# Attention on one core: value matmuls of two key tiles in one burst, and the quad sums in a shared four-bank ring

## The chip, the cores and the metric

The kernel runs on one core of one Trainium2 chip. The metric is the device time of one execution in microseconds (us); three executions of the kernel before took 3316.76, 3317.17 and 3322.76 us, with a median of 3317.17 us.

## The reference

Two conditional blocks run one after the other on x of shape (2, 2048, 512): a state space layer with a feed-forward block, then a 16-head self-attention block with conditional layer norms. Only the attention is touched here:

```python
B, N, D = hidden.shape                       # 2, 2048, 512
hd = D // num_heads                          # 16 heads of 32
h = _sln(hidden, w, ln_g, ln_b, Wg, bg, Wb, bb)
qkv = (h @ Wqkv.T + bqkv).reshape(B, N, num_heads, hd, 3)
energy = jnp.einsum('bhqd,bhkd->bhqk', q, k)
att = jax.nn.softmax(energy, axis=-1) / D ** 0.5
out = jnp.einsum('bhqk,bhkd->bhqd', att, v)
out = out @ Wp.T + bp
h1 = out + hidden
return _sln(h1, w, ...) + h1
```

## The kernel before, in words

The program is a row of stages: preparation, state space, feed-forward, query/key/value projection, attention, output projection. The attention stage (`attention_stage`, L1381) starts at about 1434 us and ends at about 3160 us of the profile.

It works through 32 blocks. A block is a group of four heads (`HG`), one of the two batches and a chunk of 512 queries (`CH`). It walks over 16 key tiles of 128 keys (`NKT`), so there are 512 tiles in all. Per tile:

- TensorE makes four scores (`score`, L1563), one per head, 128 keys by 512 queries, each in one of three PSUM banks (`SC`). A fourth score waits until ScalarE has read the first.
- ScalarE exponentiates each score into `probs` in SBUF (L1639; six tile buffers, `NPROB`).
- TensorE multiplies the exponentials of two tiles ago (`AV_LAG` = 2) with the values (`weigh`, L1575): four matmuls with 32 output columns each, side by side in the four column groups, that add up in PSUM bank `OUT` over the block. The profile shows each of these plain f32 matmuls as two instructions.
- GpSimd adds the exponentials of two tiles (`pair`, L1727), and a DMA on its queue that adds into its target folds two pairs into a quad (L1734). Nine tiles after the first tile of a quad (`SUM_LAG`), TensorE multiplies the quad with a matrix of ones (`total`, L1586), again four narrow matmuls, that add up in PSUM bank `DEN`. These are the sums of the softmax.

For the block that follows, TensorE also searches the maximum of each query's scores: `search` (L1548) makes 64 score tiles of 128 queries by 512 keys per block, in a ring of three PSUM banks (`MX`), and VectorE reduces each to a column (`find`, L1664). A search that needs a bank waits until the reduction three before it is done. After the last, the maxima are reduced (L1669), turned by TensorE (`turn`, L1554) and negated by VectorE (`negate`, L1674); the negated row goes with the queries as a further row of the score matmul. The searches run ahead of the scores: five a tile over the first twenty tiles and four a tile from there (`searched`), so the last 21 tiles have none.

The order of TensorE's work is written out: per tile score, search, score, search, `weigh` of two tiles before (and `total`, where one is due), score, search, score, search. Once a block, ScalarE copies `OUT` to SBUF (`copy_out`, L1624, in the second tile of the following block) and `DEN` to SBUF (`copy_sums`, L1629); VectorE turns the sums, inverts them and turns them back (L1681, L1685, L1689, after the finds of tiles 7, 8 and 9); GpSimd multiplies (L1715), and SyncE stores (L1487). The engines wait for each other by counting semaphores only.

Of the kernel before, what the change touches and what calls it, by code (L numbers as in the profile page):

```python
# [1380 lines left out]
def attention_stage(nc, sb, sem, psum, a, ident, wp, first, q_dram, k_dram, v_dram, att_dram):  # L1381
# [16 lines left out]
    MAXES = HG * TT * NKC  # L1398
    UNITS = HG * NKT

    AV_LAG, SUM_LAG = 2, 9
    RATE, AHEAD, TURN_KT = 4, 20, 12
    FIRST_TURN = 14

# [6 lines left out]
    part_max, maxima = first["part_max"], first["maxima"]  # L1411
    rows = sb("att_rows", [HG * TT, P], F32R)
    o_sum, den, att = sb("o_sum", [P, CH]), sb("den", [P, CH]), sb("att", [P, CH])
    inv = sb("den_inverse", [P, CH // HD])

    k_ld = [[sem(f"k_ld{b}{half}") for half in range(2)] for b in range(B)]
# [7 lines left out]
    o_copied, den_copied, den_turned, att_ready = (sem(n) for n in ("o_copied", "den_copied", "den_turned", "att_ready"))  # L1424
    inverted, spread = sem("den_inverted"), sem("inverse_spread")

    SC, MX, OUT, DEN = 0, 3, 6, 7

    def place(count):

# [11 lines left out]
    def searched(tile):  # L1442

        return min((RATE + 1) * tile, RATE * tile + AHEAD, MAXES * (BLOCKS - 1))

    def turn_of(tile):

        if tile == FIRST_TURN:
            return 1
        if tile % NKT == TURN_KT and 1 < tile // NKT + 1 < BLOCKS:  # L1450
            return tile // NKT + 1
        return None

    with nc.Block() as block:
# [73 lines left out]
        def _(pe):  # L1528
            items = [0]

            def ring_slot():

                number = items[0]
                items[0] += 1
                if number >= 3:
                    pe.wait_ge(max_read, number - 2)
                return psum[:, MX + number % 3, :]

            def search(s):

# [37 lines left out]

            def total(quad):

                count, r = quad // QUADS, quad % QUADS
# [27 lines left out]
            for tile in range(BLOCKS * NKT, BLOCKS * NKT + SUM_LAG):  # L1609
                if tile < BLOCKS * NKT + AV_LAG:  # L1610
                    weigh(tile - AV_LAG)
                if (tile - SUM_LAG) % 4 == 0:
                    total((tile - SUM_LAG) // 4)

        @block.scalar
        def _(act):
            act.sem_inc(o_copied, 1)
            act.sem_inc(den_copied, 1)
# [7 lines left out]
            def copy_sums(count):  # L1626

                act.wait_ge(sums_ready, QUADS * (count + 1))
                act.activation(den[:, :], psum[:, DEN, :], ACT.Copy).then_inc(den_copied, 1)  # L1629

            for tile in range(BLOCKS * NKT):
                count, kt = tile // NKT, tile % NKT
                if tile >= NPROB:
                    act.wait_ge(av_ready, tile - NPROB + 1)
                    act.wait_ge(pair_ready, (tile - NPROB) // 2 + 1)
                for h in range(HG):
                    unit = HG * tile + h
                    act.wait_ge(sc_ready, unit + 1)
                    act.activation(probs[tile % NPROB][:, h, :], psum[:, SC + unit % 3, :], ACT.Exp).then_inc(exp_ready, 1)  # L1639
                    if count > 0 and kt == AV_LAG - 1 and h == 2:  # L1640
                        copy_out(count - 1)
                if count > 0 and kt == SUM_LAG - 4:
                    copy_sums(count - 1)
            copy_out(BLOCKS - 1)
            copy_sums(BLOCKS - 1)

        @block.vector
        def _(dve):
            dve.memset(ones[:, :], float(D) ** 0.5).then_inc(consts, 1)
            items = [0]  # L1650

            def ring_slot():

                number = items[0]
                items[0] += 1
                dve.wait_ge(max_ready, number + 1)
                return psum[:, MX + number % 3, :]

            def find(s):
                count, j = s // MAXES + 1, s % MAXES  # L1660
                kc, qt, h = j // (HG * TT), j // HG % TT, j % HG
                if j == 0 and count > 1:
                    dve.wait_ge(max_final, count - 1)
                dve.tensor_reduce(part_max[:, h * TT + qt, kc:kc + 1], ring_slot(), AX.X, ALU.max).then_inc(max_read, 1)  # L1664
                if j == MAXES - 1:
                    dve.wait_ge(max_read, items[0])
                    if count > 1:
                        dve.wait_ge(neg_ready, count - 1)
                    dve.tensor_reduce(maxima[:, 0:HG * TT], part_max[:, :, :], AX.X, ALU.max).then_inc(max_final, 1)  # L1669

            def negate(count):
                if count > 1:
                    dve.wait_ge(row_ld, 16 * (count - 1))
                dve.tensor_scalar(rows[:, :], ring_slot()[0:HG * TT, 0:P], -1.0, None, ALU.mult).then_inc(neg_ready, 1)  # L1674
                dve.wait_ge(neg_ready, count)
                dve.sem_inc(max_read, 1)

            def turn_sums(count):
                dve.wait_ge(den_copied, count + 2)
# [12 lines left out]
            for tile in range(BLOCKS * NKT):  # L1692
                count, kt = tile // NKT, tile % NKT
                if turn_of(tile) is not None:
                    negate(turn_of(tile))
                for s in range(searched(tile), searched(tile + 1)):
                    find(s)
                if count > 0 and kt == 7:
                    turn_sums(count - 1)
                if count > 0 and kt == 8:  # L1700
                    invert(count - 1)
                if count > 0 and kt == 9:
                    spread_inverse(count - 1)
            turn_sums(BLOCKS - 1)
            invert(BLOCKS - 1)
            spread_inverse(BLOCKS - 1)

        @block.gpsimd
        def _(pool):
# [315 lines left out]
```

## Time and profile before

| | |
|---|---|
| median of three executions | 3317.17 us (3316.76 to 3322.76) |
| span of the profiled execution, from its first to its last instruction | 3319.1 us |
| TensorE matmuls busy | 3080.5 us (93%), 15333 instructions |
| VectorE busy | 2030.3 us (61%) |
| ScalarE busy | 1549.5 us (47%) |
| GpSimd busy | 1715.2 us (52%) |
| VectorE: searches reduced (L1664) | 1984, 681 ns each |
| ScalarE: exponentials (L1639) | 2048, 597 ns each |
| GpSimd: pair additions (L1727) | 256, 4580 ns each |
| TensorE: value matmuls (L1575) | 4096 instructions, 605 ns each |
| TensorE: sum matmuls (L1586) | 1024 instructions, 596 ns each |

The profile gives no time for the profiled execution apart from its span. Instructions of one engine overlap in part: four exponentials of 0.60 us each can lie within 2.11 us. So starts and ends are the safer reading, and for TensorE the starts alone, since the ends of its matmuls are modelled. In a row, "x4" joins that many instructions that follow each other.

### The profile page before, as it was taken

The numbers are of one execution on the slowest core, as the hardware profiler recorded it, in microseconds if no ns is written. First come the engines' busy times: TensorE is split into PE (matmuls) and PEld (weight loads), VectorE is DVE, ScalarE is ACT, GpSimd is POOL, SyncE is SP. The second block draws the span as 40 slices with busy tenths as digits, with TensorE's granted clock in tenths as the row PEclk, the third lists the DMA queues.
The fourth block names the chain that finished last, engine by engine and source line by source line (L and its number), as shares of the span: only waits on it lengthen the run. The fifth ranks groups of instructions, "written<-read, shape, count | busy, mean of one in ns | idle before, by whom it ended". The sixth has DMA issues, their size and how long they took to land. (4 is left out here: it accounts for less than half of the span.)

```text
span 3319.1 us, 42021 instructions
## 1 busy us (share of the span) xinstructions
PE 3080.5 (93%) x15333; PEld 1944.4 (59%) x15333; DVE 2030.3 (61%) x3514; ACT 1549.5 (47%) x2770; POOL 1715.2 (52%) x698
## 2 busy tenths in 40 slices
PE   4786999999998898989999999999999999999876
PEld 2665778777777676755454455544454554545355
DVE  7885222222221544668777777777777777777158
ACT  2232222222222232246666666666666666666622
POOL 2665301111110110137777777777777777777845
PEclk7887999999999899999999999999999999999988
DMA  6223100000000446364456654467444665444444
GB/s 239 98 102 119 40 26 25 25 25 25 25 13 16 169 171 181 115 170 101 95 106 145 147 110 91 102 143 156 96 102 102 147 132 115 102 94 97 99 169 151
DMA packets 134808, 347.68 MB, mean 105 GB/s; under 512 B 10295, under 2 KB 28219, under 8 KB 117866
## 3 DMA queue, kind: packets, MB, share of 16 engines
q1 hardware_dynamic: 116204, 211.20, 21.1%
q0 software_dynamic: 18432, 134.23, 19.9%
q8 instruction: 103, 1.69, 0.2%
q14 instruction: 69, 0.57, 0.1%
HBM read 135.34 MB, written 75.53 MB: 64 GB/s over the span
## 5 line engine op out<-in xcount | busy, mean ns | idle before, releaser
L1664 DVE TENSOR_REDUCE part_max<-psum 128x1 f32<-128x512 f32 x1984 | 1240.1, 681 | 356.2 <-PE psum L1548 350.6
L1727 POOL TENSOR_TENSOR pair<-probs 128x2048 f32<-128x2048 f32 x256 | 1172.6, 4580 | 393.0 <-ACT probs L1639 392.8
L1639 ACT ACTIVATE probs<-psum 128x512 f32<-128x512 f32 x2048 | 1090.7, 597 | 588.4 <-PE psum L1563 585.2
L1563 PE MATMUL psum<-queries,keys 97*128 97x512 f32 x2048 | 864.1, 425 | 9.4 <-PEq L1128 5.2
L1548 PE MATMUL psum<-keys,queries 96*128 96x512 f32 x1984 | 797.0, 402 | 5.4 <-DMA queries<-q_parts 5.4
L1563 PEld LDWEIGHTS psum<-queries,keys 97*128 97x128 f32 x2048 | 386.3, 189 | 501.1 <-ACT probs L1639 326.7
L1575 PE MATMUL psum<-probs,values 128*32 128x512 f32 x4096 | 545.4, 605 | 0.0
L1548 PEld LDWEIGHTS psum<-keys,queries 96*128 96x128 f32 x1984 | 376.8, 190 | 108.4 <-DVE part_max L1664 35.7
L980 DVE TENSOR_TENSOR h_lo<-w_stage,h_hi 128x512 fp32r<-128x512 f32 x128 | 96.8, 756 | 528.3 <-ACT h_hi L918 528.3
L1024 POOL TENSOR_TENSOR ffn_u_lo<-ffn_u,ffn_u_hi 128x512 fp32r<-128x512 f32 x32 | 41.2, 1287 | 554.0 <-DVE ffn_u_hi L970 554.0
L911 ACT ACTIVATE w_stage<-psum,b_col 128x512 f32<-128x512 f32 x128 | 88.1, 689 | 510.4 <-PE psum L38 510.4
L36 PE MATMUL psum<-ffn_u_hi,w_hi 128*128 128x512 f32 x512 | 203.9, 398 | 6.4 <-DVE b_parts L1006 6.4
L36 PE MATMUL psum<-w_hi,h_hi 128*128 128x512 f32 x512 | 203.5, 398 | 0.0
L38 PE MATMUL psum<-ffn_u_lo,w_hi 128*128 128x512 f32 x512 | 202.9, 396 | 0.0
L37 PE MATMUL psum<-ffn_u_hi,w_lo 128*128 128x512 f32 x512 | 202.9, 396 | 0.0
L37 PE MATMUL psum<-w_hi,h_lo 128*128 128x512 f32 x512 | 202.8, 396 | 0.0
L38 PE MATMUL psum<-w_lo,h_hi 128*128 128x512 f32 x512 | 202.2, 395 | 0.0
L1575 PEld LDWEIGHTS psum<-probs,values 128*32 128x32 f32 x4096 | 80.6, 108 | 179.3 <-issue 165.0
L1371 POOL TENSOR_TENSOR qkv_u_lo<-qkv_u,qkv_u_hi 128x512 fp32r<-128x512 f32 x32 | 41.2, 1287 | 263.7 <-DVE qkv_u_hi L1316 263.7
L1586 PE MATMUL psum<-pair,att_ones 128*32 128x512 f32 x1024 | 134.3, 596 | 13.5 <-DMA pair<-pair 13.5
L1734 POOL DMA_DIRECT2D pair<-pair x128 | 110.8, 865 | 45.5 <-POOL pair L1727 35.9
L1266 ACT ACTIVATE qk_hi<-psum,bqkv_col 128x512 fp32r<-128x512 f32 x64 | 44.0, 688 | 168.4 <-PE psum L38 151.6
(312 smaller groups left out, 3700.0 us busy)
## 6 DMA issues: line engine op xcount, KB each, us to landing
pair<-pair POOLq DMA_DIRECT2D x128, 1024.0 KB, 7.0
queries<-q_parts SPq DMA_DIRECT2D x96, 256.0 KB, 4.8
keys<-k_parts SPq DMA_DIRECT2D x42, 512.0 KB, 7.3
x<-in_x_dram SPq DMA_DIRECT2D x8, 1024.0 KB, 7.4
y<-in_x_dram SPq DMA_DIRECT2D x8, 1024.0 KB, 5.6
y_rows<-y SPq DMA_DIRECT2D x8, 1024.0 KB, 5.1
qkv_z<-z_rows SPq DMA_DIRECT2D x8, 1024.0 KB, 5.8
q_parts<-qk_hi SPq DMA_DIRECT2D x32, 256.0 KB, 2.1
```

The costliest lines, as they stand in the source:

```text
L36: nc.tensor.matmul(out, w_hi, x_hi, start=first, stop=False)
L37: nc.tensor.matmul(out, w_lo, x_hi, start=False, stop=False)
L38: return nc.tensor.matmul(out, w_hi, x_lo, start=False, stop=last)
L980: dve.tensor_tensor(h_lo[j % NH][:, :], g[j % 2], h_hi[j % NH][:, :].bitcast(F32), ALU.subtract).then_inc(glo_ready, 1)
L1548: nc.tensor.matmul(ring_slot(), queries[count % NQ][0:R, h, qt * P:(qt + 1) * P], keys[b][0:R, h, kc * CH:(kc + 1) * CH], start=True, stop ...
L1563: nc.tensor.matmul(psum[:, SC + unit % 3, :], keys[place(count)[0]][0:R + 1, h, kt * P:(kt + 1) * P], queries[count % NQ][0:R + 1, h, :], ...
L1575: mm = nc.tensor.matmul(psum[h * HD:(h + 1) * HD, OUT, :], values[b][:, kt, h * HD:(h + 1) * HD], probs[tile % NPROB][:, h, :], start=(kt ...
L1586: mm = nc.tensor.matmul(psum[h * HD:(h + 1) * HD, DEN, :], ones[:, :], pair[(2 * quad + 1) % NPAIR][:, h, :], start=(r == 0), stop=(r == Q ...
L1639: act.activation(probs[tile % NPROB][:, h, :], psum[:, SC + unit % 3, :], ACT.Exp).then_inc(exp_ready, 1)
L1664: dve.tensor_reduce(part_max[:, h * TT + qt, kc:kc + 1], ring_slot(), AX.X, ALU.max).then_inc(max_read, 1)
L1727: pool.tensor_tensor(pair[number % NPAIR][:, :, :], probs[2 * number % NPROB][:, :, :], probs[(2 * number + 1) % NPROB][:, :, :], ALU.add) ...
L1734: pool.dma_start(pair[number % NPAIR][:, :, :], pair[(number - 1) % NPAIR][:, :, :], accum_op=ALU.add).then_inc(folded, 16)
```

## The change

```diff
-    AV_LAG, SUM_LAG = 2, 9
+    AV_LAG, SUM_LAG = 3, 11
+    DIRECT = QUADS * BLOCKS - 2
+    summed = sb("summed", [P, CH])
-    SC, MX, OUT, DEN = 0, 3, 6, 7
+    SC, MX, OUT = 0, 3, 7
+    NMX = 4
 (ring_slot of TensorE)
-                if number >= 3:
-                    pe.wait_ge(max_read, number - 2)
-                return psum[:, MX + number % 3, :]
+                if number >= NMX:
+                    pe.wait_ge(max_read, number - NMX + 1)
+                return psum[:, MX + number % NMX, :]
 (total)
-                pe.wait_ge(folded, 16 * (quad + 1))
-                if r == 0:
-                    pe.wait_ge(den_copied, count + 1)
-                for h in range(HG):
-                    mm = nc.tensor.matmul(psum[h * HD:(h + 1) * HD, DEN, :], ones[:, :], pair[(2 * quad + 1) % NPAIR][:, h, :],
-                                          start=(r == 0), stop=(r == QUADS - 1))
+                direct = quad >= DIRECT
+                if not direct:
+                    pe.wait_ge(folded, 16 * (quad + 1))
+                    addends = [pair[(2 * quad + 1) % NPAIR]]
+                elif quad < QUADS * BLOCKS - 1:
+                    pe.wait_ge(pair_ready, 2 * quad + 2)
+                    addends = [pair[2 * quad % NPAIR], pair[(2 * quad + 1) % NPAIR]]
+                else:
+                    pe.wait_ge(pair_ready, 2 * quad + 1)
+                    pe.wait_ge(exp_ready, UNITS * BLOCKS)
+                    addends = [pair[2 * quad % NPAIR], probs[(4 * quad + 2) % NPROB], probs[(4 * quad + 3) % NPROB]]
+                slot = ring_slot()
+                for n, addend in enumerate(addends):
+                    for h in range(HG):
+                        mm = nc.tensor.matmul(slot[h * HD:(h + 1) * HD, :], ones[:, :], addend[:, h, :],
+                                              start=(n == 0), stop=(n == len(addends) - 1))
 (order of TensorE's work in a tile, after the second search)
-                        if tile >= AV_LAG:
-                            weigh(tile - AV_LAG)
-                        if tile >= SUM_LAG and (tile - SUM_LAG) % 4 == 0:
-                            total((tile - SUM_LAG) // 4)
-                        for s in found[HG:]:
-                            search(s)
+                        if tile % 2 == 1 and tile >= AV_LAG:
+                            weigh(tile - 3)
+                            weigh(tile - 2)
+                        if quad_of(tile) is not None:
+                            total(quad_of(tile))
+                for s in found[HG:]:
+                    search(s)
 (after the last tile)
+            weigh(BLOCKS * NKT - 2)
+            total(QUADS * BLOCKS - 2)
+            weigh(BLOCKS * NKT - 1)
+            total(QUADS * BLOCKS - 1)
 (ScalarE: copy_sums and its calls are gone; VectorE)
+            def gather(quad):
+                count, r = quad // QUADS, quad % QUADS
+                dve.wait_ge(sums_ready, quad + 1)
+                slot = ring_slot()
+                if r == 0:
+                    if count > 0:
+                        dve.wait_ge(den_turned, count)
+                    dve.tensor_copy(summed[:, :], slot).then_inc(max_read, 1)
+                else:
+                    dve.wait_ge(max_read, last_sum[0])
+                    dve.tensor_tensor(summed[:, :], slot, summed[:, :], ALU.add).then_inc(max_read, 1)
+                last_sum[0] = items[0]
-                dve.transpose(att[:, :], den[:, :]).then_inc(den_turned, 1)
+                dve.transpose(att[:, :], summed[:, :]).then_inc(den_turned, 1)
+                for s in found[0:2]:
+                    find(s)
+                if quad_of(tile) is not None:
+                    gather(quad_of(tile))
+                for s in found[2:]:
+                    find(s)
 (GpSimd: the last pair is not added, the last two quads are not folded)
-            for number in range(PAIRS * BLOCKS):
+            for number in range(PAIRS * BLOCKS - 1):
-                if p % 2 == 1:
+                if p % 2 == 1 and quad < DIRECT:
```

Here `quad_of(tile)` is the quad whose sum is due in a tile: `(tile - 11) // 4` where `tile % 4 == 3`, from tile 11 on. The values are weighed in the odd tiles, two tiles at a time. The quad sum goes into the next bank of the ring, which now has four banks, and VectorE adds it to `summed` in SBUF, between the second and the third find of the tile.

## Rows read from the trace of the kernel before

**Rows 1.** Busy us of PE, PEld, DVE, ACT, POOL in 500 us; clock, DMA.
```profile
1500.00:2000.00 500.00, 498.83 (x2716) 248.97 (x2715) 391.11 (x649) 326.05 (x619) 387.49 (x122) 1.00 0.55 116
```
**Rows 2.** Waits, 1500 to 3100 us: who for whom, us in total, times, longest.
```profile
ACT probs L1639 <- PE psum L1563: 548.8, 481, 3.5
DVE part_max L1664 <- PE psum L1548: 338.7, 415, 3.1
PEld psum L1586 <- DMA pair<-pair: 9.1, 6, 2.3
```
**Rows 3.** Timeline of TensorE: start, us, engine, line, operation; tiles in steady state.
```profile
2001.44 1.06 PE L1575 MATMUL psum<-probs,values 128*32 128x512 f32 x8
2002.44 0.50 PE L1563 MATMUL psum<-queries,keys 97*128 97x512 f32 x1
2002.78 0.40 PE L1548 MATMUL psum<-keys,queries 96*128 96x512 f32 x1
...
2004.19 0.39 PE L1548 MATMUL psum<-keys,queries 96*128 96x512 f32 x1
2004.51 1.07 PE L1575 MATMUL psum<-probs,values 128*32 128x512 f32 x8
...
2010.64 1.06 PE L1575 MATMUL psum<-probs,values 128*32 128x512 f32 x8
...
2014.56 1.06 PE L1575 MATMUL psum<-probs,values 128*32 128x512 f32 x8
```
**Rows 4.** Timeline of ScalarE and VectorE after the first of these bursts.
```profile
2002.98 2.11 ACT L1639 ACTIVATE probs<-psum 128x512 f32<-128x512 f32 x4 [0.51 <-PE psum L1563]
2003.21 2.48 DVE L1664 TENSOR_REDUCE part_max<-psum 128x1 f32<-128x512 f32 x4 [0.58 <-PE psum L1548]
```
**Rows 5.** Timeline of ScalarE where it copies the block's output.
```profile
1986.81 0.60 ACT L1639 ACTIVATE probs<-psum 128x512 f32<-128x512 f32 x1 [1.81 <-PE psum L1563]
...
1987.78 1.59 ACT L1639 ACTIVATE probs<-psum 128x512 f32<-128x512 f32 x3
```
**Rows 6.** Timeline of VectorE where it turns the sums.
```profile
2007.48 0.70 DVE L1681 STREAM_TRANSPOSE att<-den 128x512 f32<-128x512 f32 x1
2008.11 2.52 DVE L1664 TENSOR_REDUCE part_max<-psum 128x1 f32<-128x512 f32 x4
```
**Rows 7.** Timeline around the turn of the maxima, TensorE and VectorE.
```profile
2017.62 1.06 PE L1575 MATMUL psum<-probs,values 128*32 128x512 f32 x8
...
2020.59 0.27 DVE L1674 TENSOR_SCALAR att_rows<-psum 16x128 fp32r<-16x128 f32 x1
...
2021.01 1.29 DVE L1664 TENSOR_REDUCE part_max<-psum 128x1 f32<-128x512 f32 x2
2021.16 1.06 PE L1575 MATMUL psum<-probs,values 128*32 128x512 f32 x8
```
**Rows 8.** Groups by line and shape, VectorE additions and products in other stages.
```profile
L632 DVE TENSOR_TENSOR prod<-scan,s_sin 128x512 f32<-128x512 f32 x16 | 27.2, 1699 | 0.0
L1905 DVE TENSOR_TENSOR p_h<-psum,p_z 128x512 f32<-128x512 f32 x32 | 20.9, 685 | 29.5 <-PE psum L38 29.3 <-issue 0.2
```
**Rows 9.** Timeline of TensorE in the last block, which has no searches.
```profile
3126.32 0.96 PE L1563 MATMUL psum<-queries,keys 97*128 97x512 f32 x3
...
3127.51 0.49 PE L1563 MATMUL psum<-queries,keys 97*128 97x512 f32 x1 [0.23 <-ACT probs L1639]
...
3127.93 1.06 PE L1575 MATMUL psum<-probs,values 128*32 128x512 f32 x8
```
**Rows 10.** Timeline of the end of the attention stage.
```profile
3140.89 2.08 PE L1575 MATMUL psum<-probs,values 128*32 128x512 f32 x16
...
3141.93 4.52 POOL L1727 TENSOR_TENSOR pair<-probs 128x2048 f32<-128x2048 f32 x1 [0.42 <-ACT probs L1639]
...
3153.75 1.94 PE L1586 MATMUL psum<-pair,att_ones 128*32 128x512 f32 x8 [8.83 <-DMA pair<-pair]
3155.76 0.60 ACT L1629 ACTIVATE den<-psum 128x512 f32<-128x512 f32 x1 [12.13 <-PE psum L1586]
```

More of the change, by code:

```diff
@@ L1423, in attention_stage @@
     max_ready, max_read, max_final, neg_ready = (sem(n) for n in ("max_ready", "max_read", "max_final", "neg_ready"))
-    o_copied, den_copied, den_turned, att_ready = (sem(n) for n in ("o_copied", "den_copied", "den_turned", "att_ready"))
+    o_copied, den_turned, att_ready = (sem(n) for n in ("o_copied", "den_turned", "att_ready"))
     inverted, spread = sem("den_inverted"), sem("inverse_spread")
-    SC, MX, OUT, DEN = 0, 3, 6, 7
+    SC, MX, OUT = 0, 3, 7
+    NMX = 4
     def place(count):
@@ L1444, in searched, with quad_of @@
         return min((RATE + 1) * tile, RATE * tile + AHEAD, MAXES * (BLOCKS - 1))
+    def quad_of(tile):
+        return (tile - SUM_LAG) // 4 if tile >= SUM_LAG and (tile - SUM_LAG) % 4 == 0 else None
     def turn_of(tile):
@@ L1579, in total @@
             def total(quad):
-                count, r = quad // QUADS, quad % QUADS
-                pe.wait_ge(folded, 16 * (quad + 1))
-                if r == 0:
-                    pe.wait_ge(den_copied, count + 1)
-                for h in range(HG):
-                    mm = nc.tensor.matmul(psum[h * HD:(h + 1) * HD, DEN, :], ones[:, :], pair[(2 * quad + 1) % NPAIR][:, h, :],
-                                          start=(r == 0), stop=(r == QUADS - 1))
+                direct = quad >= DIRECT
[14 more added lines that the diff above has]
+                                              start=(n == 0), stop=(n == len(addends) - 1))
                 mm.then_inc(sums_ready, 1)
@@ L1602, in _ @@
                     if h == 1:
-                        if tile >= AV_LAG:
-                            weigh(tile - AV_LAG)
-                        if tile >= SUM_LAG and (tile - SUM_LAG) % 4 == 0:
-                            total((tile - SUM_LAG) // 4)
-                        for s in found[HG:]:
-                            search(s)
[L1609 to L1613, printed above, removed]
+                        if tile % 2 == 1 and tile >= AV_LAG:
[9 more added lines that the diff above has]
+            total(QUADS * BLOCKS - 1)
         @block.scalar
@@ L1617, in _ @@
             act.sem_inc(o_copied, 1)
-            act.sem_inc(den_copied, 1)
             def copy_out(count):
@@ L1624, in copy_out @@
                 act.activation(o_sum[:, :], psum[:, OUT, :], ACT.Copy).then_inc(o_copied, 1)
-            def copy_sums(count):
-                act.wait_ge(sums_ready, QUADS * (count + 1))
-                act.activation(den[:, :], psum[:, DEN, :], ACT.Copy).then_inc(den_copied, 1)
             for tile in range(BLOCKS * NKT):
@@ L1639, in _ @@
                     act.activation(probs[tile % NPROB][:, h, :], psum[:, SC + unit % 3, :], ACT.Exp).then_inc(exp_ready, 1)
-                    if count > 0 and kt == AV_LAG - 1 and h == 2:
+                    if count > 0 and kt == 1 and h == 2:
                         copy_out(count - 1)
-                if count > 0 and kt == SUM_LAG - 4:
-                    copy_sums(count - 1)
             copy_out(BLOCKS - 1)
-            copy_sums(BLOCKS - 1)
         @block.vector
@@ L1649, in _, with max_slot @@
             dve.memset(ones[:, :], float(D) ** 0.5).then_inc(consts, 1)
-            items = [0]
+            items, maxed, last_sum = [0], [0], [0]
             def ring_slot():
-                number = items[0]
                 items[0] += 1
-                dve.wait_ge(max_ready, number + 1)
-                return psum[:, MX + number % 3, :]
+                return psum[:, MX + (items[0] - 1) % NMX, :]
+            def max_slot():
+                maxed[0] += 1
+                dve.wait_ge(max_ready, maxed[0])
+                return ring_slot()
             def find(s):
@@ L1663, in find @@
                     dve.wait_ge(max_final, count - 1)
-                dve.tensor_reduce(part_max[:, h * TT + qt, kc:kc + 1], ring_slot(), AX.X, ALU.max).then_inc(max_read, 1)
+                dve.tensor_reduce(part_max[:, h * TT + qt, kc:kc + 1], max_slot(), AX.X, ALU.max).then_inc(max_read, 1)
                 if j == MAXES - 1:
@@ L1673, in negate @@
                     dve.wait_ge(row_ld, 16 * (count - 1))
-                dve.tensor_scalar(rows[:, :], ring_slot()[0:HG * TT, 0:P], -1.0, None, ALU.mult).then_inc(neg_ready, 1)
+                dve.tensor_scalar(rows[:, :], max_slot()[0:HG * TT, 0:P], -1.0, None, ALU.mult).then_inc(neg_ready, 1)
                 dve.wait_ge(neg_ready, count)
                 dve.sem_inc(max_read, 1)
+            def gather(quad):
[10 more added lines that the diff above has]
+                last_sum[0] = items[0]
             def turn_sums(count):
-                dve.wait_ge(den_copied, count + 2)
+                dve.wait_ge(max_read, last_sum[0])
                 dve.wait_ge(att_st, 16 * (count + 1))
-                dve.transpose(att[:, :], den[:, :]).then_inc(den_turned, 1)
+                dve.transpose(att[:, :], summed[:, :]).then_inc(den_turned, 1)
             def invert(count):
@@ L1693, in _ @@
                 count, kt = tile // NKT, tile % NKT
+                found = range(searched(tile), searched(tile + 1))
                 if turn_of(tile) is not None:
                     negate(turn_of(tile))
-                for s in range(searched(tile), searched(tile + 1)):
+                for s in found[0:2]:
[3 more added lines that the diff above has]
+                for s in found[2:]:
                     find(s)
@@ L1703, in _ @@
                     spread_inverse(count - 1)
+            gather(QUADS * BLOCKS - 2)
+            gather(QUADS * BLOCKS - 1)
             turn_sums(BLOCKS - 1)
```

## The prediction

> **What bounds the kernel now.** I read the busy time of a stretch of the attention stage first, because that stage holds 1700 of the 3319 us and all that is changed. TensorE is busy 498.8 of 500 us there at the full granted clock, and VectorE, ScalarE and GpSimd 391, 326 and 387 us [rows 1]. The waits come second: ScalarE waits 549 us for scores and VectorE 339 us for search tiles, both for TensorE [rows 2]. So what TensorE does per tile sets the time.
>
> Third, the timeline of one tile, by starts alone, shows what this is. From one value burst to the next are 3.07 us, and the average over three is 9.20 / 3 = 3.067. From the burst's start to the next score are 1.00 us, from that score to the last search 1.75 us, and then 0.32 us to the next burst; score and search together take (2004.19 - 2002.78) / 3 = 0.47 us [rows 3]. Four such pairs are 1.88 us, so a burst adds 3.067 - 1.88 = 1.19 us to a tile. But a tile whose burst also holds the sum matmuls takes 14.56 - 10.64 = 3.92 us: a second group of the same shape adds only 0.853 us. The difference, 1.19 - 0.85 = 0.33 us, is paid once for each burst, for going from full-width matmuls to those of 32 columns and back.
>
> A block of 16 tiles is 12 x 3.067 + 4 x 3.92 = 52.5 us. The turn of the maxima makes one tile 3.54 us long in place of 3.07 [rows 7], so it costs 0.47, which gives 53.0 us. As a check, the 2716 TensorE instructions in 500 us, at 64 + 64 + 128 + 32 + 1 = 289 a block, give 53.2 us [rows 1].
>
> **The change, part by part.** *Two tiles in a burst.* Number and size of the matmuls stay. A stretch from burst to burst has eight scores and eight searches now: 0.33 + 2 x 0.853 + 8 x 0.47 = 5.80 us against 6.13 us, and 6.65 with a sum (due in tiles 3, 7, 11 and 15, all odd, so no sum has a burst of its own). Saved: 0.333 us per two tiles, 0.667 per quad. With four searches a tile this holds for tiles 20 to 490, 117.8 quads: **-78.5 us**.
>
> *Do ScalarE and VectorE keep up over a stretch twice as long?* Take the stretch's first score as 0. Scores start at 0.10 + 0.47k (k = 0 starts at 0), searches at 0.34 + 0.47k. ScalarE starts 0.54 us after the first score and takes (2.11 - 0.60) / 3 = 0.50 us per exponential; VectorE starts 0.43 us after the first search, at 0.77, and takes (2.48 - 0.68) / 3 = 0.60 us per reduction [rows 3, 4]. So exponential k ends at 1.14 + 0.50k and reduction k at 1.45 + 0.60k. Score 7 needs exponential 4, which ends at 3.14, and is due at 3.39. Search 7 needs, with four banks, reduction 3, at 3.25, and is due at 3.63. With about 0.06 us for the semaphore, my estimate from the 0.05 us between an exponential's end and a waiting score in the last block [rows 9], neither waits. With three banks the search would have waited 0.28 us, so the fourth bank is needed.
>
> *The quad sum in the ring.* VectorE gets 128 instructions, each an addition or copy of 128x512 from PSUM. The nearest row is the addition of a PSUM and an SBUF tile, 0.685 us [rows 8]; 16 reductions and one of them are 10.3 us of a quad's 12.45. The sum is the last thing of its burst, which by its modelled end is done 0.06 us after the next score starts (2001.44 + 1.06 against 2002.44), so VectorE starts it at about 0.12 and ends at 0.81, and the first reduction was only due at 0.77: the burst hides the addition. Cost 0, if it isn't longer and the sum isn't seen later; both are priced below. The bank is next needed by the fourth search, at 1.75, which is later.
>
> A page bears on this. In "SBUF — State Buffer", section "Who interferes with whom", the Trainium skill says that a VectorE instruction whose two inputs both lie in SBUF contends with GpSimd for a read port, and one with a single SBUF input doesn't. By that rule the addition here, with one input in PSUM, keeps its 0.685 us; the trace agrees in the two rows of that group, where `p_h`, with one input in PSUM, takes 0.685 and a product of two SBUF tiles 1.70. Without the rule the sum would be that of the contention rival below.
>
> *Stalls that the longer stretch brings.* What sits between reductions now delays a search that nothing else separates from it. (a) The turned sums and the turned inverse hold VectorE 0.63 us each (2008.11 - 2007.48) [rows 6], both after the second reduction of a stretch: reduction 3 ends at 3.88, search 7 starts at 3.94 in place of 3.63, 0.31 us each, twice a block, in 30 blocks: **+18.6**. Today such a stall does not show. (b) `copy_out` sits behind the first exponential of a stretch and moves the next to 0.97 us after it [rows 5]; exponential 4 ends at 3.62, score 7 starts at 3.67 in place of 3.39: 0.28 x 30 = **+8.4**. Bounds for both: 0, as today, and for (a) the full 0.63, +38. (c) The turn costs 0.47 us in a ring of three. In the changed kernel the negation (0.42 us with what follows it, 2021.01 - 2020.59 [rows 7]) comes after two reductions, so reduction 3 ends at 3.67, and with the turn in the ring search 7 is due at about 3.74: no wait, and I leave 0.10 us for the turn itself: 0.37 x 29 = **-11** (bounds 0 and -13.6).
>
> *The early tiles.* With ten searches in 5.80 + 0.47 = 6.27 us, search 9 waits for reduction 5 (4.51) and is due at about 4.12: 0.39 us lost against 0.33 gained. **0**.
>
> *The last 21 tiles* have no searches and go by ScalarE. The fourth score starts 1.19 us into the stretch, 0.05 after the first exponential's end, and the burst 0.42 after it [rows 9]. With eight: score 7 at 0.54 + 4 x 0.50 + 0.60 + 0.05 = 3.2, burst at 3.6, next stretch 1.00 + 0.85 later, at 5.48, against 2 x (1.61 + 1.00) = 5.22. Ten such stretches: **+2.6**.
>
> *Fold.* A quad is used 11 tiles after its first, not 9, which gives the DMA some 6 us more; today TensorE waits 9.1 us for it in all [rows 2]. Since part of that is idle weight load alone, I take **-4**, bounds 0 and -9. GpSimd has 2 x 4.6 us of additions and 1.2 of DMA issue in 12.45, so it keeps up; the even pair after a fold just fits (starts at 7.5 us, the fold's issue ends at 7.45).
>
> *ScalarE's copy of the sums* goes, 31 x 0.5 us that nobody waited for; 0.
>
> *The end.* Today the last pair is added from 3141.93 on, folded, multiplied at 3153.75 and read at 3155.76 [rows 10]. Now TensorE goes on from 3140.89: values of one tile and two groups of ones for quad 126 (3 x 0.853, to 3143.45), values of the last tile and three groups for quad 127 (4 x 0.853, to 3146.86); pair 254 is ready by about 3142. The last group ends 0.2 us later by its modelled length, and VectorE reads at 3147.13, in place of ScalarE at 3155.76; what follows is the same. **-8.6**, the three extra groups of direct addends included.
>
> **Sum:** -78.5 + 18.6 + 8.4 - 11 + 2.6 - 4 - 8.6 = -72.5 us. From the profiled execution's 3319.1 us that makes 3246.6. Its span lies 1.9 above the median 3317.17 and inside the three times, so I apply the difference to the median: 3244.7, say **3245 us**.
>
> **Rivals.** *Sum seen late (3282).* VectorE sees the sum not at 0.12 but at about 0.7 us, as long after the burst as ScalarE's first exponential is after its score. The first reduction then starts at 1.32, search 7 at 3.86: 0.23 us in 88 stretches, and 0.58 in the 30 where the sums are also turned: +37. For it: all stretches with a sum have no slack before the first reduction. Against: after the last burst ScalarE reads 0.07 us after the modelled end (3153.75 + 1.94, 3155.76) [rows 10].
>
> *No new stalls (3213).* VectorE's helper work is absorbed as today, the fold's wait goes whole: 3245 - 27 - 5. Against: the arithmetic of the ring above; for: the last 0.3 us of each stretch may hide part of it.
>
> *The addition contends with GpSimd (3331, slower).* GpSimd adds pairs in 78% of the time [rows 1]. If the addition takes the 1.70 us of the row with two SBUF inputs [rows 8] in place of 0.685, the first reduction starts at 1.75 and search 7 at 4.29, 0.66 late; in the stretches with turned sums 0.98 more than the 0.31: 88 x 0.66 + 30 x 0.98 = 87, less 1. It stalls from about 1.1 us on and eats the whole gain from about 1.6. Against: `p_h` in that group has its operands in the same places as this addition, and takes 0.685 over 32 instructions.
>
> *The 0.33 us doesn't go (about 3320).* It belongs to each tile's group of values, not to the change of width: -78.5 falls away, 3245 + 78.5 = 3323, less some of the stalls that a slower stretch hides. Against: the sum's group, appended to the values', shows no such cost.
>
> The page "TensorEngine Tiling (Array Packing)", section "Performance Considerations", has a rule of the Trainium skill that speaks against the change: after packing, reading PSUM can become the limit, and both ScalarE and VectorE should do it. Here the reading of sums goes from ScalarE, the emptier one, to VectorE. By the rows VectorE has 10.3 of 12.45 us a quad, so I count it as the late-sum rival and no more.
>
> **How the numbers follow.** Forecast 60%, its own range 3230 to 3262; late sum 17%; no new stalls 11%; contention 6%; no saving per burst 6%. The range takes the forecast, all but the far end of the no-stall case and the late sum: 3218 to 3286. A difference within 0.2%, 6.6 us, can't be told from none. Faster: 60 + 17 + 11 + 2 (half-way cases of the last two) = 90%; same 4%; slower 6%.
>
> **What would show it.** Value bursts in pairs, 256 of them, each pair 1.00 + 0.85 us from its start to the next score; 5.80 and 6.65 us from burst to burst; blocks of 49.8 us and stalls, about 51 us. The addition at about 0.69 us, starting within 0.2 us of the next score. In the waits, search behind `find` grows to some 20 us in place of the turn's wait, and score behind exponential appears once a block. The time between the last exponential and the store about 8.6 us shorter. It is wrong if bursts come at 6.1 us, or if searches wait in every stretch with a sum.

## The result, and the profile after

The changed kernel takes 3261.63 us (median of four runs, 3259.81 to 3263.84), the kernel before beside it 3319.97 us (3316.76 to 3326.12). The ratio is 0.9821, with a 95% interval of 0.9807 to 0.9835: about 58 us faster. The forecast was 3245 us and a gain of 72.5; the time is 17 us above it, the gain 14 us short, and the range 3218 to 3286 holds the time.

500 us of the attention stage, in the columns of [rows 1]:
```profile
1500.00:2000.00 500.00, 498.95 (x2816) 267.76 (x2815) 424.24 (x714) 322.14 (x630) 399.61 (x126) 1.00 0.56 119
```
TensorE is as full as before, but does 2816 instructions where it did 2716. At 289 a block that is 51.3 us a block against 53.2. VectorE has gone from 391 to 424 us: 27 of the 33 us are quad sums (four of 0.69 us a block), the rest are more reductions in the same time.

The waits of 1500 to 3050 us, which answer to [rows 2]:
```profile
ACT probs L1649 <- PE psum L1570: 543.2, 246, 3.0
...
DVE summed L1699 <- PE psum L1602: 125.1, 91, 10.6
DVE part_max L1675 <- PE psum L1555: 95.3, 119, 1.0
...
PEld psum L1555 <- DVE part_max L1675: 39.0, 132, 0.4
...
PEld psum L1570 <- ACT probs L1649: 39.0, 138, 0.8
...
PEld psum L1602 <- DMA pair<-pair: 0.3, 1, 0.3
```
and one row of the kernel before, over the same window:
```profile
PEld psum L1548 <- DVE part_max L1664: 21.0, 66, 0.8
```
TensorE is still what everybody waits for. The wait for the fold has gone from 9.1 to 0.3 us. Searches waited for VectorE's reductions before, too, 21 us in 66 weight loads; now it is 39 us in 132. Weight loads of scores wait 39 us for exponentials, about four times a block; most of these are in the stretch in which ScalarE copies the output.

A plain stretch with a sum, TensorE alone, which answers to [rows 3]:
```profile
2015.98 1.92 PE L1582 MATMUL psum<-probs,values 128*32 128x512 f32 x16
2017.72 1.04 PE L1602 MATMUL psum<-pair,att_ones 128*32 128x512 f32 x8
2018.69 0.50 PE L1570 MATMUL psum<-queries,keys 97*128 97x512 f32 x1
...
2022.27 0.39 PE L1555 MATMUL psum<-keys,queries 96*128 96x512 f32 x1
2022.59 1.92 PE L1582 MATMUL psum<-probs,values 128*32 128x512 f32 x16
```
From burst to burst are 6.61 us for two tiles and a sum, where [rows 3] give 3.07 + 3.92 = 6.99: sixteen value instructions in one burst, one step in and one step out, no wait between. Over most blocks a stretch with a sum is 6.64 to 6.74 us (6.67 typical) and one without 5.77 to 5.89 (5.82). The eight gaps of a typical block, from the value burst of tile 3 on: 6.67, 5.82, **7.05**, **6.19**, **6.87**, 5.82, 6.66, **6.15**. The bold ones are the stretches with the turned sums (tile 7), the turned inverse (9), the turn of the maxima (11) and the copied output (tile 1 of the next block).

The first of these, TensorE and VectorE, with ScalarE's and GpSimd's rows, the scores behind the first and most weight loads (PEld) left out; it answers to [rows 6]:
```profile
1992.76 0.50 PE L1570 MATMUL psum<-queries,keys 97*128 97x512 f32 x1
1992.90 0.69 DVE L1699 TENSOR_TENSOR summed<-psum,summed 128x512 f32<-128x512 f32 x1 [1.14 <-PE psum L1602]
...
1993.54 1.29 DVE L1675 TENSOR_REDUCE part_max<-psum 128x1 f32<-128x512 f32 x2
...
1994.74 0.70 DVE L1705 STREAM_TRANSPOSE att<-summed 128x512 f32<-128x512 f32 x1
...
1995.22 0.19 PEld L1555 LDWEIGHTS psum<-keys,queries 96*128 96x128 f32 x1
1995.37 2.45 DVE L1675 TENSOR_REDUCE part_max<-psum 128x1 f32<-128x512 f32 x4
1995.45 0.40 PE L1555 MATMUL psum<-keys,queries 96*128 96x512 f32 x1
...
1996.07 0.19 PEld L1555 LDWEIGHTS psum<-keys,queries 96*128 96x128 f32 x1 [0.42 <-DVE part_max L1675]
1996.07 0.51 PE L1555 MATMUL psum<-keys,queries 96*128 96x512 f32 x1
...
1996.67 0.50 PE L1555 MATMUL psum<-keys,queries 96*128 96x512 f32 x1
...
1997.10 1.92 PE L1582 MATMUL psum<-probs,values 128*32 128x512 f32 x16
```
The addition starts 0.14 us after the stretch's first score and takes 0.69, so the first reduction starts where it would have without it. The transposition then moves the rest by 0.6 us, and the last two searches, 1996.07 and 1996.67, wait for their banks: they come 0.60 us apart, at VectorE's pace, in place of 0.47. The weight load of a search that doesn't wait starts 0.23 us before it (1995.22 for 1995.45); that of the one that waits starts with it (1996.07).

The end of the stage, which answers to [rows 10]:
```profile
3091.64 1.06 PE L1582 MATMUL psum<-probs,values 128*32 128x512 f32 x8
3092.52 1.90 PE L1602 MATMUL psum<-pair,att_ones 128*32 128x512 f32 x16
3094.24 1.04 PE L1582 MATMUL psum<-probs,values 128*32 128x512 f32 x8
...
3095.96 1.90 PE L1602 MATMUL psum<-probs,att_ones 128*32 128x512 f32 x16
3097.93 0.69 DVE L1699 TENSOR_TENSOR summed<-psum,summed 128x512 f32<-128x512 f32 x1 [2.74 <-PE psum L1602]
```
From the last value burst's start to the reading of the last sum are 6.29 us, where they were 3155.76 - 3140.89 = 14.87.

### The profile page after: what moved, and what is told of

Same layout as the page of the kernel before. It is cut to its first block and busy times, and to the rows that moved or that the text cites. A ratio compares the mean times of both kernels' runs of the same rounds, so it can differ in the third digit from the quotient of the medians.

```text
span 3262.1 us, 42381 instructions
## 1 busy us (share of the span) xinstructions
PE 3030.3 (93%) x15357; PEld 1980.8 (61%) x15357; DVE 2100.3 (64%) x3642; ACT 1500.3 (46%) x2738; POOL 1707.9 (52%) x695
## 5 line engine op out<-in xcount | busy, mean ns | idle before, releaser
L1649 ACT ACTIVATE probs<-psum 128x512 f32<-128x512 f32 x2048 | 1053.2, 612 | 583.5 <-PE psum L1570 581.1
L1675 DVE TENSOR_REDUCE part_max<-psum 128x1 f32<-128x512 f32 x1984 | 1218.8, 680 | 111.4 <-PE psum L1555 105.9
L1570 PE MATMUL psum<-queries,keys 97*128 97x512 f32 x2048 | 850.7, 417 | 8.3 <-PEq L1128 5.2
L1582 PE MATMUL psum<-probs,values 128*32 128x512 f32 x4096 | 494.3, 600 | 0.0
L980 DVE TENSOR_TENSOR h_lo<-w_stage,h_hi 128x512 fp32r<-128x512 f32 x128 | 105.9, 827 | 522.0 <-ACT h_hi L918 522.0
L1582 PEld LDWEIGHTS psum<-probs,values 128*32 128x32 f32 x4096 | 107.2, 109 | 234.1 <-ACT probs L1649 136.2
L1699 DVE TENSOR_TENSOR summed<-psum,summed 128x512 f32<-128x512 f32 x96 | 66.4, 692 | 165.7 <-PE psum L1602 165.7
```

The costliest lines, as they stand in the source:

```text
L980: dve.tensor_tensor(h_lo[j % NH][:, :], g[j % 2], h_hi[j % NH][:, :].bitcast(F32), ALU.subtract).then_inc(glo_ready, 1)
L1570: nc.tensor.matmul(psum[:, SC + unit % 3, :], keys[place(count)[0]][0:R + 1, h, kt * P:(kt + 1) * P], queries[count % NQ][0:R + 1, h, :], ...
L1582: mm = nc.tensor.matmul(psum[h * HD:(h + 1) * HD, OUT, :], values[b][:, kt, h * HD:(h + 1) * HD], probs[tile % NPROB][:, h, :], start=(kt ...
L1675: dve.tensor_reduce(part_max[:, h * TT + qt, kc:kc + 1], max_slot(), AX.X, ALU.max).then_inc(max_read, 1)
```

## The experiments

All ratios are to the kernel before, run on the same chip. Gaps are from value burst to value burst in the profile. Edits are to the changed kernel where nothing else is said, and the diffs show their main lines.

**Two halves of the change.** `e2_single_bursts`: everything but the pairing.
```diff
-    AV_LAG, SUM_LAG = 3, 11
+    AV_LAG, SUM_LAG = 2, 11
-                        if tile % 2 == 1 and tile >= AV_LAG:
-                            weigh(tile - 3)
-                            weigh(tile - 2)
+                        if tile >= AV_LAG:
+                            weigh(tile - AV_LAG)
```


> The changed kernel with the values weighed in every tile again (two tiles late), all else kept: four-bank ring, sums added in SBUF by VectorE, no fold at the end. Theory: 512 bursts instead of 256, each 0.33 us: +78.5 us over the tiles with four searches; the stalls of the long stretches go (0.40 twice, 0.35 and 0.12 us a block in the profile of the changed kernel, 30 blocks: -38), the last tiles give -3. About 3299 us, value bursts 3.07 us apart without a stall. Rival 1 (0.33 us belongs to each group of values, not to a burst): the bursts cost nothing more and the time falls to about 3222 us. Rival 2 (stalls of the long stretch are not from its length): they stay, 3337 us.

Measured: 3296.59 us, ratio 0.9930 (0.9915 to 0.9946). A plain tile of it:
```profile
2039.90 1.06 PE L1582 MATMUL psum<-probs,values 128*32 128x512 f32 x8
...
2042.97 1.07 PE L1582 MATMUL psum<-probs,values 128*32 128x512 f32 x8
```
3.07 us a tile again, as in [rows 3], and no search waits for VectorE in the waits of 1500 to 3050 us. The 0.33 us belong to the burst, and the stalls to the long stretch. A rival falls with each. The tile with the turn of the maxima, which also has a sum, takes 4.03 us here against 3.93 for others with a sum: with four banks the turn costs 0.10 us.

`e8_pairs_only`: the pairing alone, on the kernel before, with its three banks for the maxima and its own bank for the sums. The diff leaves out that VectorE turns and inverts the sums one tile later, and the order behind the last tile.
```diff
-    AV_LAG, SUM_LAG = 2, 9
+    AV_LAG, SUM_LAG = 3, 11
-                        if tile >= AV_LAG:
-                            weigh(tile - AV_LAG)
+                        if tile % 2 == 1 and tile >= AV_LAG:
+                            weigh(tile - 3)
+                            weigh(tile - 2)
```


> The kernel before with the pairing alone: values of two tiles in one burst, sums 11 tiles late, but a ring of three banks for the maxima, the sums adding up in their own PSUM bank and copied by ScalarE, the fold up to the end; VectorE's work on the sums sits one tile later than in the kernel before. Ring theory: 0.667 us saved per quad, but 0.28 us lost in each of eight stretches of a block, and the turn and the copies cost what they did or some tenths more: a block of about 52.8 us against 53.2, -12 us in all, -4 for the fold's wait, +6 at the start and +3 in the last tiles: about 3313 us. Rival (pairing pays without the fourth bank): about 3265 us.

Measured: 3344.11 us, ratio 1.0073 (1.0057 to 1.0088): slower than before, and 31 us above what I expected. The sign of the theory was right and its size too small: the plain gaps are 6.19 and 7.05 us, 0.38 above the 5.82 and 6.67 of the four-bank kernel, not 0.28.

`e1_three_banks` takes the fourth bank from the changed kernel.
```diff
-    NMX = 4
+    NMX = 3
```


> The changed kernel with one edit: the ring that maxima and quad sums share has three banks instead of four. Ring theory: between two bursts lie eight searches now; with three banks search 7 waits for reduction 4 (ends 3.85 us after the stretch's first score, plus 0.06 for the semaphore) and is due at 3.63, so each plain stretch grows by 0.28 us; the stretches in which VectorE also turns sums, spreads inverses or negates maxima grow by about 0.5 more than with four banks, the first twenty tiles by 0.6 us per two tiles. About 2.6 us per block over 30 blocks and 5 at the start: 3345 us, slower than the kernel before. Rival (the burst alone pays, the fourth bank only serves the turn of the maxima): at most 14 us more, 3275 us.

Measured: 3365.15 us, ratio 1.0134 (1.0119 to 1.0150), 20 us above what I expected; the rival is out. The stretch, TensorE alone, shows where the missing 0.1 us is:
```profile
2058.13 0.39 PE L1555 MATMUL psum<-keys,queries 96*128 96x512 f32 x1
...
2060.50 0.50 PE L1555 MATMUL psum<-keys,queries 96*128 96x512 f32 x1
...
2061.10 0.50 PE L1555 MATMUL psum<-keys,queries 96*128 96x512 f32 x1
...
2061.70 0.50 PE L1555 MATMUL psum<-keys,queries 96*128 96x512 f32 x1
2062.13 1.92 PE L1582 MATMUL psum<-probs,values 128*32 128x512 f32 x16
```
The last search comes 3.57 us after the first, where seven pairs of 0.47 are 3.29: the 0.28 of the theory. But the burst comes 0.43 us after it, not 0.32. A search that has waited is followed by a longer gap (its modelled length is 0.50 instead of 0.40, and the score after it comes 0.34 us later and not 0.24). So a stretch that ends in a wait costs 0.1 us more than the wait. For eight stretches and 30 blocks that makes, as an estimate, 24 us in `e8_pairs_only`, most of its miss. The first score behind a burst has the same marks in [rows 3] (0.50 us long, the search 0.34 us after it). What both have in common in the trace is a weight load that starts with its matmul; that this is the cause was not tried.

**The end alone.** `e3_end_only`, on the kernel before:
```diff
-            for number in range(PAIRS * BLOCKS):
+            for number in range(PAIRS * BLOCKS - 1):
-                if p % 2 == 1:
+                if p % 2 == 1 and quad < DIRECT:
(total with direct addends as in the changed kernel, into the bank DEN)
```


> The kernel before with the new end alone: the last pair is not added and the last two quads are not folded, their parts are multiplied with the ones directly into the sums' bank. Theory: the last sum is read 8.6 us earlier and nothing else moves: 3311.4 us. Rival (the three extra groups or a colder clock in the following stage eat it): no change, 3320 us.

Measured: 3310.80 us, ratio 0.9970 (0.9959 to 0.9981). From the last value burst of the tiles to ScalarE's copy of the sums are 6.29 us (3139.89 to 3146.18), 8.6 less than before.

**Where VectorE's and ScalarE's side work sits.** `e4_copy_later`:
```diff
-                    if count > 0 and kt == 1 and h == 2:
+                    if count > 0 and kt == 2 and h == 2:
```


> The changed kernel with ScalarE's copy of the block's output moved from behind the first exponential of a stretch to behind the fifth (third tile of the block, third head). Theory: the stretch from tile 1 to tile 3 takes 6.15 us in the profile of the changed kernel against 5.82 for a plain one, because the copy delays exponential 4 and so score 7; behind the fifth it delays none: -0.33 us in 31 blocks, 10 us, 3251 us. Rival (something else at the block's begin, such as its first score or the value bank, makes that stretch long): no change, 3262 us, or more where the next value burst waits for the copy.

Measured: 3249.95 us, ratio 0.9788 (0.9775 to 0.9802). The 6.15 us gap is 5.81, and all others are as they were. The copy's delay was there, but not first at score 7. In the changed kernel, in a stretch whose first score starts at 1973.30:
```profile
1974.33 0.59 ACT L1639 ACTIVATE o_sum<-psum 128x512 f32<-128x512 f32 x1
...
1975.46 0.19 PEld L1570 LDWEIGHTS psum<-queries,keys 97*128 97x128 f32 x1 [0.46 <-ACT probs L1649]
1975.47 0.51 PE L1570 MATMUL psum<-queries,keys 97*128 97x512 f32 x1
```
This is score 4, at 2.17 us where it was due at 1.98 by the prediction's formula; it waits for exponential 1, the next behind the copy.

`e5_turns_later`:
```diff
-                if count > 0 and kt == 7:      # turn_sums
+                if count > 0 and kt == 8:
-                if count > 0 and kt == 8:      # invert
+                if count > 0 and kt == 9:
-                if count > 0 and kt == 9:      # spread_inverse
+                if count > 0 and kt == 12:
-                if p == 5 and count > 0:       # GpSimd's product
+                if p == 6 and count > 0:
```


> The changed kernel with VectorE's turning of the sums moved from behind the second reduction of a stretch (after tile 7) to behind the sixth (after tile 8), the inverse after tile 9, and its turning from after tile 9 to after tile 12; GpSimd multiplies one pair later. Theory: search 7 waits for reduction 3, which these no longer delay: the two stretches of 7.05 and 6.19 us come back to 6.66 and 5.82: -0.76 us in 30 blocks, 23 us, 3239 us. Rival (VectorE's load as such sets it, 85% of the time busy): the stall moves to the stretches where they now sit, 3262 us.

Measured: 3237.54 us, ratio 0.9746 (0.9731 to 0.9760). The gaps of 7.05 and 6.19 us are 6.67 and 5.82, and none of the others has grown. VectorE has the same work; only its place in the stretch counts.

`e6_both_later` has both edits.

> Both moves together. Theory: they are in different stretches and on different engines and add up: 3262 - 10 - 23 = 3229 us, blocks of about 50.1 us. Rival (they compete, because what is won in one stretch is lost waiting in another): no better than the better one of the two.

Measured: 3228.93 us, ratio 0.9721 (0.9708 to 0.9735), and once more, as `e11_both_later_again`, beside the two kernels below:

> The kernel of e6 once more, unchanged, as the measure for the two others on the same chip: 3229 us within 3.

Measured: 3232.27 us, ratio 0.9728 (0.9715 to 0.9742). They add up. TensorE's row for 500 us:
```profile
1500.00:2000.00 500.00, 499.99 (x2866) 278.30 (x2866) 433.94 (x731) 329.52 (x647) 409.52 (x130) 1.00 0.57 120
```
2866 instructions, 50.4 us a block.

**How much the burst hides.** `e7_two_additions`:
```diff
+                    (waits for its own previous addition into `extra`)
+                    dve.tensor_tensor(extra[:, :], slot, summed[:, :], ALU.add).then_inc(extra_done, 1)
                     dve.tensor_tensor(summed[:, :], slot, summed[:, :], ALU.add).then_inc(max_read, 1)
```


> The changed kernel in which VectorE makes the addition of a quad sum twice, once into an unused tile (96 additions of 0.69 us more; the 32 copies stay single). Theory: the second addition is no longer hidden by the burst: the first reduction starts at about 1.4 us instead of 0.77 after the stretch's first score, so search 7 waits about 0.3 us more in 66 plain stretches and 0.6 more in the 30 that also turn the sums: about 35 to 40 us, 3299 us. Rival (VectorE has slack in the whole stretch, and one more instruction of 0.7 us hides): 3262 us. If the addition were already unhidden, it would cost its full 0.62 us each, 60 us: 3321 us.

Measured: 3300.11 us, ratio 0.9936 (0.9921 to 0.9951). The plain gap with a sum grows from 6.67 to 7.01, the one with turned sums from 7.05 to 7.61. The first 0.69 us are free, and of the second about half is paid in a plain stretch and nearly all where the slack is already spent:
```profile
2042.51 0.50 PE L1571 MATMUL psum<-queries,keys 97*128 97x512 f32 x1
2042.65 0.69 DVE L1703 TENSOR_TENSOR extra<-psum,summed 128x512 f32<-128x512 f32 x1 [1.50 <-PE psum L1603]
...
2043.26 0.68 DVE L1704 TENSOR_TENSOR summed<-psum,summed 128x512 f32<-128x512 f32 x1
...
2043.85 4.27 DVE L1676 TENSOR_REDUCE part_max<-psum 128x1 f32<-128x512 f32 x7
```

**The ends of the stage, and the turn.** `e9_single_at_ends`, on top of e6:
```diff
+    PAIRED = 20, NKT * (BLOCKS - 1) - 2
+                        if 2 <= tile < PAIRED[0] or tile >= PAIRED[1]:
+                            weigh(tile - 2)
-                        if tile % 2 == 1 and tile >= AV_LAG:
+                        elif tile % 2 == 1 and tile >= AV_LAG:
```
(the output is copied in the second tile of the second and the last block, in the third of the others)

> The version with both moves (e6), but with single bursts where pairs don't pay: in the first 20 tiles, with five searches a tile, and in the last block, without searches (there the output's copy stays behind the second tile's third exponential). Theory: the first tiles take 6.61 us per two again instead of 6.79, -1.5 us; the last eighteen 11.3 us per quad instead of 11.7, -2 us; and the value burst of 3.4 us at a granted clock of 0.57, seen once in the last block of the changed kernel, goes, -1.6 us: about 5 us less than e6, 3224 us. Rival (the ends don't matter, or the clock falls all the same): no change against e6.

Measured: 3220.22 us (3218.15 to 3222.10), ratio 0.9695 (0.9682 to 0.9708), the fastest version. That is 12 us below `e11_both_later_again`, run beside it, but the stages before differ by scatter (first score at 1434.7 against 1443.6 us), so the stage's own length is the better measure: from its first score to the last sum 1619 us against 1624 and 1625 in the two profiles of the e6 kernel, the 5 us of the theory. The first tiles are 3.30 us apart again, the last ones 2.61 and 3.47 with a sum, and none of the value bursts there is of low clock.

`e10_turn_later`, on top of e9:
```diff
-    RATE, AHEAD, TURN_KT = 4, 20, 12
+    RATE, AHEAD, TURN_KT = 4, 20, 13
```


> The version e9 with the turn and the negation of the maxima one tile later, so that they come before the seventh search of a stretch instead of the third. Theory: the stretch that holds them takes 6.88 us against 6.67 for a plain one with a sum; the negation no longer delays reduction 3, the turn's own 0.1 us stays: -0.1 us in 29 blocks, 3 us less than e9. Rival (the time is the turn's own, in TensorE): no change.

Measured: 3223.91 us, ratio 0.9710 (0.9697 to 0.9723): no gain, and the gap grows from 6.88 to 7.05. I had forgotten that the turn takes a bank. Placed before search 6, it makes search 7 wait for reduction 4 instead of 3, due at 3.91 us with the semaphore, against 3.63 plus the turn's 0.1:
```profile
2039.37 0.27 PE L1562 MATMUL psum<-ident,maxima 128*16 128x128 f32 x1
2039.40 0.48 PE L1571 MATMUL psum<-queries,keys 97*128 97x512 f32 x1
2039.78 0.50 PE L1556 MATMUL psum<-keys,queries 96*128 96x512 f32 x1
2040.12 0.39 PE L1571 MATMUL psum<-queries,keys 97*128 97x512 f32 x1
2040.38 0.49 PE L1556 MATMUL psum<-keys,queries 96*128 96x512 f32 x1
```
These are TensorE's rows alone. Both searches behind the turn wait, again 0.60 us apart.

## Why the prediction was right, and where it was 14 us off

The terms, from the value burst of tile 21 to that of tile 493 (29.5 blocks), and the ends:

| Step | predicted, us | measured, us | from |
|---|---|---|---|
| bursts in pairs, with the fold's wait | -78.5 - 4 | -82.3 | 29.5 x (53.22 - 0.47 - 49.96) |
| turned sums and inverse | +18.6 | +22.1 | 29.5 x (0.38 + 0.37) |
| copied output | +8.4 | +9.7 | 29.5 x 0.33 |
| turn of the maxima | -11 | -7.7 | 29.5 x (0.21 - 0.47) |
| quad sum on VectorE | 0 | 0 | addition at 0.14 us, 0.69 us long |
| first tiles | 0 | +1.0 | tile 3 to tile 21 |
| last tiles and end | +2.6 - 8.6 | -3.9 | tile 493 to the reading of the last sum |
| rest | 0 | -1.2 | half before tile 3, half in the blocks |
| whole stage | -72.5 | -62.3 | 1717.3 to 1654.9 us, first score to last sum |

Here 53.22 us is the mean block before and 49.96 four plain gaps of each kind after.

*The price of a burst*, the largest term, was right: of the 82.3 us about 78 are the bursts' (typical tiles of 3.07 and 3.93 us against the 49.96) and about 4 the fold's, and `e2_single_bursts` shows that the price is the burst's. The page "TensorEngine Tiling (Array Packing)" of the Trainium skill, section "Key Properties", says that a change of tiling mode drains TensorE, without a price; a price of 0.33 us for the way in and out fits that. But that it is the change of width is not shown: at each burst the kernel also goes from matmuls of type f32r (`queries`, `keys`) to plain f32 (`probs`, `values`, the ones) and back, and no run takes the two apart.

*The hidden addition* was right: 0.692 us against 0.685; the contention rival is out as a forecast, and so is the late sum (0.14 us, not 0.7). `e7_two_additions` shows that it was hidden by little. But for the contention the changed kernel is a weak test. GpSimd is busy 400 of 500 us, yet 88 of the 96 additions of its profile lie where GpSimd runs nothing, between two pair additions. A better one is in `e9_single_at_ends`, where three additions lie wholly inside a pair addition, among them this one:
```profile
1770.00 4.87 POOL L1761 TENSOR_TENSOR pair<-probs 128x2048 f32<-128x2048 f32 x1
1773.76 0.69 DVE L1702 TENSOR_TENSOR summed<-psum,summed 128x512 f32<-128x512 f32 x1 [1.12 <-PE psum L1603]
```
They take 0.692 us as well. The rule of the Trainium skill ("SBUF — State Buffer", "Who interferes with whom") that one input in SBUF doesn't contend with GpSimd held there. The 1.70 us of the rival was a mean that hides the mechanism. In the kernel before the sixteen products behind it (`s_sin`, two SBUF inputs) take 0.68 to 1.79 us; the 0.68 is the one that GpSimd was idle beside, and the others (typically 1.76) start while a GpSimd instruction runs. Products of the same line and shape with `s_cos`, two SBUF inputs too, take 0.68 us; all but one have GpSimd beside them as well, but start before its instruction:
```profile
109.30 0.68 DVE L632 TENSOR_TENSOR prod<-scan,s_cos 128x512 f32<-128x512 f32 x1
109.45 1.68 POOL L664 TENSOR_TENSOR y<-gated,y 128x512 f32<-128x512 f32 x1 [1.74 <-DVE gated L609]
109.90 1.78 DVE L632 TENSOR_TENSOR prod<-scan,s_sin 128x512 f32<-128x512 f32 x1
```
In these rows it is who comes first that decides, and not the inputs alone.

*The stalls* were placed right, each in its stretch. Moving the side work takes those of the copied output and of the turned sums and inverse away whole (`e4_copy_later`, `e5_turns_later`); that of the turn stays. Their size was too small, 0.31 against 0.38, 0.28 against 0.33, 0.10 against 0.21 us. The step that failed is the sentence that search 7 starts at 3.94 and the stretch grows by the difference. The start was right (3.91 us), but TensorE loses about 0.1 us more behind a wait, which `e1_three_banks` shows in every stretch. For the turn the 0.10 us left for it is what `e2_single_bursts` measures; what failed is "no wait". In the turn's stretch whose first score starts at 2262.15 us, search 7 starts at 3.74 us, when reduction 3 has just ended (3.68), and the burst comes 0.42 us later instead of 0.32. The weight load of that search shows the wait:
```profile
2265.89 0.18 PEld L1555 LDWEIGHTS psum<-keys,queries 96*128 96x128 f32 x1 [0.25 <-DVE part_max L1675]
```
For the copied output the prediction looked at score 7 alone, and score 4 is the first to wait (`e4_copy_later`); that the size came out near is in part luck.

*The last tiles and the end.* The end's 8.6 us were right (14.87 to 6.29, and again in `e3_end_only`). The last tiles were not: one value burst there took 1.65 us more than its like, at a low clock, which no row of before had.

*Outside the stage* the profiled run of the changed kernel is 5.3 us longer, 4.5 of them before the stage (first score at 1443.00 us against 1438.49). The code there is the same, and the first scores of all profiled runs lie between 1434.7 and 1443.7, and two executions of one and the same kernel, `e6_both_later` and `e11_both_later_again`, have them at 1438.7 and 1443.6, so I read it as scatter between executions. That and the stage's 10 us make the gain of the profiled execution 57.0 us where 72.5 were forecast; by medians it is 58.3.

The rival "no new stalls" (3213 us) is out as a forecast, but e6 with 3229 us comes within 16 us of it: most of what the stalls cost could be had back, by moving five lines.

## What to carry to other kernels

Where full-width and narrow matmuls alternate, count the bursts and price one by comparing a tile with one narrow group to a tile with two. A longer stretch between bursts moves the need for banks: work out, for each engine that empties them, when the last matmul of the stretch is due and which reading it waits for, and place the emptying engine's other work behind the reading that matters. The two halves of this change need each other: the pairing without the fourth bank lost 0.7%, the rest without the pairing won 0.7%, and both together won 1.8%.

## What the runs showed of the hardware

In the last block, where TensorE has waits for ScalarE in every tile, the granted clock fell in single bursts of the paired kernels. Windows around one, in the changed kernel (columns as in [rows 1]), and the burst:
```profile
3048.00:3051.00 3.00, 2.30 (x6) 0.74 (x4) 0.00 (x0) 3.00 (x7) 2.52 (x3) 1.00 0.43 87
3051.00:3055.00 4.00, 4.00 (x22) 1.09 (x25) 0.00 (x0) 1.47 (x4) 3.16 (x1) 0.57 0.98 197
3055.00:3060.00 5.00, 4.78 (x28) 1.70 (x20) 0.69 (x1) 3.62 (x8) 2.46 (x1) 1.00 0.02 3
```
```profile
3051.49 3.56 PE L1582 MATMUL psum<-probs,values 128*32 128x512 f32 x16
3054.88 1.03 PE L1602 MATMUL psum<-pair,att_ones 128*32 128x512 f32 x8
```
The sixteen instructions take 3.39 us to the sum's, against 1.74 in a plain stretch, at a mean granted clock of 0.57, close to the 1.2 GHz level. Just before, TensorE had two waits for exponentials, 0.22 and 0.48 us, around the copied output. All eight profiled kernels with pairs in the last block have one or two such bursts there (2.95 to 3.55 us to the next instruction; `e8_pairs_only` and `e11_both_later_again` two), and the five with single bursts there, `e9_single_at_ends` among them, none. What exactly lets the clock fall was not tried apart from that.
